# Storing a layer's output earlier, and moving work between PE, VectorE and ScalarE, in a four-layer convolution kernel

## What is computed

```python
x = x + _L0_conv_ref(_gn(x), w_real, w_imag, b_real, b_imag)  # rfft2, complex 3x3 convolution over frequencies, irfft2
x = x + _L1_conv_ref(_gn(x))                                  # gates each row by the sign of a product with column sums
x = x + _L2_conv_ref(_gn(x), L2_conv_W)                       # 3x3 convolution, 16 to 16 channels
x = x + _L3_conv_ref(_gn(x), L3_conv_weight)                  # 3x3 convolution, 16 to 16 channels
```

## Time and profile before

| what | value |
|---|---|
| runs | 4728.77, 4733.0 and 9641.31 us, median 4733.0 |
| profiled execution | 4716.25 us, span 4714.5 us |
| PE busy | 4226.5 us, 90% of the span |
| DVE busy | 3331.8 us, 71% |
| ACT busy | 2541.0 us, 54% |
| DMA | 467.98 MB, mean 99 GB/s; written to HBM 134.22 MB |
| granted PE clock, mean | 0.959 of full speed |

### The profile page before, as it was taken

The page is one execution under the profiler, slowest core; times in us unless marked ns, Lnnn a source line. Parts: engine busy times, 40 slices in busy tenths (PEclk is TensorE's granted clock), DMA queues, the critical chain, the costliest instruction groups (busy, mean ns, idle before and its releaser), DMA issues.

```text
span 4714.5 us, 229091 instructions
## 1 busy us (share of the span) xinstructions
PE 4226.5 (90%) x84848; PEld 2660.6 (56%) x84848; DVE 3331.8 (71%) x13348; ACT 2541.0 (54%) x8637; POOL 1.0 (0%) x6
## 2 busy tenths in 40 slices
PE   4898989989899898998989989899898999988799
PEld 1455765556555566555655556555665556655476
DVE  1887658876588665887658876588756887578873
ACT  4675526655267542775437754377533675335552
POOL 0000000000000000000000000000000000000000
PEclk8999999989999899999999999999999998999999
DMA  7442015520156202661026610356003560034304
GB/s 190 128 136 77 4 40 179 186 82 4 43 184 188 73 4 56 185 187 60 3 66 189 187 46 3 87 184 189 28 3 104 181 185 18 3 99 140 96 4 146
DMA packets 290241, 467.98 MB, mean 99 GB/s; under 512 B 25536, under 2 KB 92288, under 8 KB 289408
## 3 DMA queue, kind: packets, MB, share of 16 engines
q1 hardware_dynamic: 289536, 457.92, 32.2%
HBM read 323.60 MB, written 134.22 MB: 97 GB/s over the span
## 4 chain that ended last, share of the span: by engine, by line
PE 60%; DVE 12%; DMA 8%; issue 8%; SPq 5%; ACT 3%; DVEq 1%; ACTq 1%
PE ps L1352 35%; PE ps L1255 9%; DMA raw<-x 8%; PE ps L1270 4%; PE ps L1263 3%; PE ps L1279 3%; PE ps L1125 2%; DVE shared L858 2%; SPq L426 2%; SPq L433 1%; DVE xin L853 1%; DVE shared L854 1%; ACT x L584 1%; SPq L407 1%; DVE shared L860 1%
## 5 line engine op out<-in xcount | busy, mean ns | idle before, releaser
L1352 PE MATMUL ps<-x,conv_s 32*32 32x512 f32 x49104 | 1753.1, 608 | 76.2 <-DVE x L1016 41.0
L1352 PEld LDWEIGHTS ps<-x,conv_s 32*32 32x32 f32 x49104 | 1246.7, 104 | 520.0 <-issue 290.2
L1255 PE MATMUL ps<-shared 32*32 32x512 f32 x16384 | 654.0, 603 | 0.0
L662 ACT ACTIVATE x<-ps,vec 128x256 f32<-128x256 f32 x512 | 214.6, 470 | 738.6 <-PE ps L1352 738.6
L1270 PEld LDWEIGHTS ps<-hil,shared 128*128 128x128 f32 x4096 | 500.3, 193 | 194.1 <-issue 193.3
L584 ACT ACTIVATE x<-ps,vec 128x128 f32 (+1 forms) x1024 | 376.7, 384 | 430.2 <-PE ps L1270 429.1
L858 DVE SCALAR_TENSOR_TENSOR shared<-xin,trig 128x128 f32<-128x128 f32 x2048 | 530.9, 299 | 106.6 <-DVE shared L854 98.8
L1279 PE MATMUL ps<-eye,vsb 128*128 128x128 f32 x2048 | 369.0, 303 | 222.5 <-DVE vsb L879 127.5
L1270 PE MATMUL ps<-hil,shared 128*128 128x128 f32 x4096 | 567.5, 282 | 0.0
L1086 DVE SCALAR_TENSOR_TENSOR x<-ps,x 128x256 f32<-128x256 f32 x512 | 214.9, 420 | 423.2 <-ACT x L662 422.3
L1255 PEld LDWEIGHTS ps<-shared 32*32 32x32 f32 x16384 | 306.9, 103 | 280.7 <-issue 217.1
(11 more groups left out here) (202 smaller groups left out, 4641.5 us busy)
## 6 DMA issues: line engine op xcount, KB each, us to landing
out<-x SPq DMA_DIRECT2D x512, 256.0 KB
shared<-x SPq DMA_DIRECT2D x448, 256.0 KB
raw<-x SPq DMA_DIRECT2D x256, 256.0 KB
raw<-x SPq DMA_DIRECT2D x512, 128.0 KB
shared<-t_strip SPq DMA_DIRECT2D x512, 96.0 KB, 4.0
x<-x SPq DMA_DIRECT2D x64, 256.0 KB, 7.9
x<-t_proj SPq DMA_DIRECT2D x1, 2048.0 KB, 13.3
trig<-t_trig SPq DMA_DIRECT2D x1, 512.0 KB, 9.9
```

Of the source, the lines that this page charges most:

```text
L1255: mm = pe.matmul(ps[TM * cg:TM * cg + TM, bank, :], wst[TM * rg:TM * rg + TM, k, v, a, :], of[TM * rg:TM * rg + TM, :], start=(a == AXS), ...
L1352: mm = pe.matmul(halves(ps[TM * cg:TM * cg + TM, banks[k], :]), conv_s[TM * rg:TM * rg + TM, kw, second, :], x1b[TM * rg:TM * rg + TM, of, ...
```

## The change

- **Stores.** `DEFERRED` goes from 56 to 8. In the third convolution SP stores 56 strips (all 64 in the last image) in a loop of four stores each; 8 strips are left for the first four pairs of the next first layer. The loads of pairs 0 and 1 of the next image still stand ahead of the stores.
- **PE.** In each step the projection stands between the odd `hilbert` and the odd `turn`, no longer behind both.
- **DVE.** `make_planes` takes the differences first, then the sums, and waits for results less strictly. `x_taken` is counted by the sums, now the second of the two.
- **copy_v.** ACT makes both copies; DVE makes none.

```diff
@@ -27,7 +27,7 @@
 GROUPS = STRIPS // GROUP
 STORE_SEMS = 4
 STORES = 16 * STRIPS // STORE_SEMS
-DEFERRED = STRIPS - 2 * UNROLL
+DEFERRED = 2 * UNROLL
 SIDE = HALF + 2
 WIDE = 2 * SIDE
 PAIRS = STRIPS // 2
@@ -416,14 +416,13 @@
             for k in range(STORE_SEMS):
                 sp.sem_inc(c_stored[k], STORES)
 
-            def store(i, s):
-
-                k = s % STORE_SEMS
+            def store(i, s, k, turn):
+
                 sp.wait_ge(evicted, ev(i, 1 + STRIPS + s + 1))
                 sp.sem_inc(s_sp, 1)
-                sp.wait_ge(c_stored[k], (i + 1) * STORES + s // STORE_SEMS * 16)
+                sp.wait_ge(c_stored[k], (i + 1) * STORES + turn * 16)
                 sp.sem_inc(s_sp, 1)
-                sp.dma_start(out[i].rearrange("c (s r) w -> s r c w", r=ROWS)[s], x1[:, s, 0:N]).then_inc(c_stored[k], 16)
+                sp.dma_start(out[i].rearrange("c (s r) w -> s r c w", r=ROWS)[s], x1[:, bass.ds(s, 1), 0:N]).then_inc(c_stored[k], 16)
 
             def load_next(image, s, t, k):
 
@@ -456,25 +455,19 @@
                     sp.sem_inc(s_sp, 1)
                 for pair in range(2, AHEAD):
                     load_pair(i, pair, 2 * pair)
-                for pair in range(DEFERRED // 2):
+                for pair in range(PAIRS):
                     feed(pair, 2 * pair % TABLES)
-                    if stores_left:
+                    if stores_left and pair < DEFERRED // 2:
                         for e in range(2):
-                            store(i - 1, STRIPS - DEFERRED + pair * 2 + e)
-                for pair in range(PAIRS - UNROLL, PAIRS):
-                    feed(pair, 2 * pair % TABLES)
+                            s = STRIPS - DEFERRED + pair * 2 + e
+                            store(i - 1, s, s % STORE_SEMS, s // STORE_SEMS)
                 if more:
                     for pair in range(2):
                         load_pair(i + 1, pair, 2 * pair)
 
-                for n in range(PAIRS):
-                    if more and n >= PAIRS - (STRIPS - DEFERRED):
-                        sp.wait_ge(evicted, ev(i, 1 + STRIPS + 2 * n + 2))
-                        sp.sem_inc(s_sp, 1)
-                        store(i, n - (PAIRS - (STRIPS - DEFERRED)))
-                    elif not more:
-                        for e in range(2):
-                            store(i, 2 * n + e)
+                with sp.Fori(0, (STRIPS - (DEFERRED if more else 0)) // STORE_SEMS) as j:
+                    for k in range(STORE_SEMS):
+                        store(i, j * STORE_SEMS + k, k, j)
 
             image(0, True, False)
             with sp.Fori(1, B - 1) as i:
@@ -588,8 +581,9 @@
                 def copy_v(pair):
 
                     act.wait_ge(mixed, i * PAIRS + pair + 1 + MIXED_CREDIT)
-                    act.wait_ge(turned, t0 + pair * 2 + T_CREDIT)
-                    nc.scalar.activation(vsb[:, 1, :], ps[:, BV + 1, :], ACT.Identity).then_inc(v_copied[1], 1)
+                    for e in range(2):
+                        act.wait_ge(turned, t0 + pair * 2 - 1 + e + T_CREDIT)
+                        nc.scalar.activation(vsb[:, e, :], ps[:, BV + e, :], ACT.Identity).then_inc(v_copied[e], 1)
 
                 def squares(s, k, uses):
 
@@ -849,17 +843,20 @@
                     dve.wait_ge(x_loaded[e], (i * PAIRS + pair + 1) * (16 + 16 * e))
                     dve.wait_ge(mixed, i * PAIRS + pair - 1 + MIXED_CREDIT)
                     plus, minus = xin[:, k, 0:HALF], xin[:, k, HALF:N]
-                    b.did(V.scalar_tensor_tensor(plus, raw[:, e, 0:HALF], v1(MEAN2), raw[:, e, HALF:N], ALU.subtract, ALU.add))
-                    V.tensor_tensor(minus, raw[:, e, 0:HALF], raw[:, e, HALF:N], ALU.subtract).then_inc(x_taken, 1)
-                    b.then(V.scalar_tensor_tensor(fg(wst[:, k]), fg(mix_s[:, 1]), row_trig[:, 0, bass.ds(s, 1)], fg(mix_s[:, 0]), ALU.mult, ALU.add))
-                    dve.wait_ge(x_taken, i * STRIPS + s + 1 + RAW)
+                    b.did(V.tensor_tensor(minus, raw[:, e, 0:HALF], raw[:, e, HALF:N], ALU.subtract))
+                    V.scalar_tensor_tensor(plus, raw[:, e, 0:HALF], v1(MEAN2), raw[:, e, HALF:N], ALU.subtract, ALU.add).then_inc(x_taken, 1)
+                    b.did(V.scalar_tensor_tensor(fg(wst[:, k]), fg(mix_s[:, 1]), row_trig[:, 0, bass.ds(s, 1)], fg(mix_s[:, 0]), ALU.mult, ALU.add))
+                    b.settle(but=1)
                     for a in range(2):
                         for q in range(2):
                             b.did(V.scalar_tensor_tensor(quarter(planes[:, a, k, :], q, 0), split_in(minus)[:, q, :], 1.0, split_in(trig[:, a, 0:HALF])[:, q, :],
                                                          ALU.mult, ALU.mult, accum_out=gsum[:, 2 * a + q, bass.ds(s, 1)]))
+                        if a == 0:
+                            dve.wait_ge(x_taken, i * STRIPS + s + 1 + RAW)
                         ins = V.tensor_tensor(planes[:, a, k, HALF:N], plus, trig[:, a, 0:HALF], ALU.mult)
                         if a == 0:
                             b.did(ins)
+                            b.settle(but=3)
                             b.did(V.scalar_tensor_tensor(fg(wst[:, k]), fg(mix_s[:, 2]), row_trig[:, 1, bass.ds(s, 1)], fg(wst[:, k]), ALU.mult, ALU.add))
                     ins.then_inc(planes_ready, 1)
                     assert b.n == DVE_B, b.n
@@ -871,12 +868,6 @@
                 c = Steps(dve, d_prep, i * DVE_PREPS)
 
                 t0 = i * STRIPS
-
-                def copy_v(pair):
-
-                    dve.wait_ge(mixed, i * PAIRS + pair + 1 + MIXED_CREDIT)
-                    dve.wait_ge(turned, t0 + pair * 2 - 1 + T_CREDIT)
-                    V.tensor_copy(vsb[:, 0, :], ps[:, BV, :]).then_inc(v_copied[0], 1)
 
                 u0 = i * (STRIPS // UNROLL)
 
@@ -892,7 +883,6 @@
 
                 def step(pair, slot, dotting=True):
 
-                    copy_v(pair)
                     make_planes(i, pair + 2, slot)
                     if dotting:
                         dots(pair - 2)
@@ -904,7 +894,6 @@
                 with dve.Fori(1, PAIRS // 2 - 1) as j:
                     step(j * 2, 0)
                     step(j * 2 + 1, 2)
-                copy_v(PAIRS - 2)
                 dve.wait_ge(b_steps, (t0 + STRIPS) * DVE_B)
                 dve.wait_ge(planes_ready, t0 + STRIPS)
                 dve.wait_ge(dotted, t0 + STRIPS - 8 + DOT_CREDIT)
@@ -918,8 +907,8 @@
                         if j == 1 or kk + 1 < KINDS:
                             c.did(ins)
                 ins.then_inc(f_ready, 1)
+                dve.wait_ge(mixed, i * PAIRS + PAIRS - 1 + MIXED_CREDIT)
                 dots(PAIRS - 4)
-                copy_v(PAIRS - 1)
                 for pair in range(PAIRS - 3, PAIRS):
                     dots(pair)
                 dve.wait_ge(dotted, t0 + STRIPS + DOT_CREDIT)
@@ -1290,10 +1279,11 @@
 
                     mix(t, odd)
                     add_u(t - 1, 1 - odd, table, table_uses)
-                    for e in range(2):
-                        hilbert(t * 2 - 2 + e, e, 1 - odd)
-                        turn(t, e)
+                    hilbert(t * 2 - 2, 0, 1 - odd)
+                    turn(t, 0)
+                    hilbert(t * 2 - 1, 1, 1 - odd)
                     project_next(2 * (1 - odd), table, uses, first)
+                    turn(t, 1)
 
                 pe.wait_ge(v_u, i + 1)
                 pe.wait_ge(a_cols, A_COLS * i + A_COLS)
```

## The result

| | before | after |
|---|---|---|
| median of four runs | 4731.45 us (4728.77 to 4733.0, and one of 9641.31) | 4901.54 us (4892.9 to 4906.85) |
| profiled span | 4714.5 us | 4903.6 us |
| granted PE clock, mean | 0.959 | 0.931 |

The ratio is 1.0352, 95% interval 1.0333 to 1.037. It leaves out the run of 9641.31 us; the two medians alone give 1.036.

A forecast was written before the change was run, and what follows sets the result against it. It took PE's steps in the first layer, with their waits, as the longest part, and SP's order as deciding the seam. Steps -195 us, seams +181, rest 0: 4733 - 14 = 4719, say 4720 us, range 4630 to 4850.

The forecast's parts named there:

- The pace of the stores: At the seam, SP's block of 56 stores: 1.17 us from one store to the next, 65.5 us in all.
- The time of a store, 4.3 us: Wait for the fourth store back: taken from the run's last store, a quarter of it giving 1.08 us a store.
- the source address by register: SP's own work in the new store loop: register addressing and the branch add 0.05 us to 1.12 us a store.
- Rival A: Dearer seam: 1.45 us or more a store through the wait for the fourth store back; 4829 us, chance 0.14.
- Rival C: Stores drain faster at the seams, 0.92 us a strip if SP issues that fast; 4621 us, chance 0.10.
- the page's sum: Seam by the Trainium skill's DMA fit: 56 strips in 34 us, seam free, near 4540 us; part of C's chance.
- The step: First layer, one pair of strips: 8.55 us once PE's waits are covered, from 9.21 and 9.52; -195 us in all.
- rival B: First layer: ScalarE becomes the bound through its second copy, 0.6 us a step; 4845 us, chance 0.06.
- the gap of 5.5 us where SP jumps back: At the seam: time from the last store's end to pair 2's load, kept as before; none from image 0 to 1.
- from SP's load to the mix 13 us: At the seam: pair 2's mix comes 13 us after SP issues its load, with 12 to 16 possible.
- the signs that were named: Profile signs: 65 us store block, steps of 8.5 to 8.7, PE still 20 to 35 at seams, ScalarE idle under 0.9.
- The rest: Outside steps and seams: -1 us an image from planes, +1 us from dense stores in the third convolution, together 0.

The follow-up runs named there:

- half_stores: The changed kernel with each store of the third convolution's loop moving only 256 of 512 columns, except in the last image; 4843.81 us, ratio 1.0229.
- eight_deep: The changed kernel with one wait for evictions per eight stores and eight store semaphores, so a store waits for the eighth before it; 4847.08 us, ratio 1.0224.
- split_wait: `rest_alone` with PE's wait for the odd strip's eviction moved from the start of the mix to its first odd matmuls; 4528.15 us, ratio 0.9554.
- unblocked: The changed kernel with 40 of the 56 stores ahead of the loads of the next image's pair 1; 4591.43 us, ratio 0.9692.
- rest_alone: The changed kernel with SP's program as before the change (`DEFERRED = 56`); 4573.69 us, ratio 0.9652.

## Why the prediction was wrong

It said 4720 us, no change; it is 4901.54, slower by 3.5%, and above the range. The account of the mechanism held: a gain in the first layer, given back at the seam behind a block of 56 stores. Two terms were mis-sized, both towards a faster kernel, and it took both to leave the range: with the seams as measured and the steps as forecast the sum is 4733 - 195 + 286 = 4824, the other way round 4733 - 107 + 181 = 4807, both inside 4630 to 4850.

**The pace of the stores, "I take 1.17".** The blocks take 78.7 to 81.1 us, 1.41 to 1.45 a store, in place of 65.5. That is 13 to 16 us at a seam and 102 in all, nearly the whole difference between +286 and +181. The prediction built the pace from two rows, and both terms were too low. The time of a store, 4.3 us, came from the very last one; with four in flight it is 5.6, which the text had only as the upper end. This term alone gives 1.40, and it did so behind image 0, where SP's own work is 1.14 us, no more than the 1.17 that was forecast. The other term, 0.05 us for "the source address by register", holds there, but behind images 1 to 6, where the image number is in a register as well, it is 0.25: 1.37 in `half_stores`. The trace before already had a loaded store in it. In the last image, with a store each 1.6 us, SP waited twice for the fourth store back, and these had been issued 5.8 and 6.3 us before:

```profile
SPq L425 <- DMA out<-x: 0.6, 2, 0.3
```

**Rival A** has the right pace (1.45) and the right mechanism behind image 0, where waits for the fourth store back make up the 0.27 us between SP's own work and the pace. Behind images 1 to 6 it is one of two limits: SP waits little (3.7 us in the block from image 1 to 2), since its own work is already at 1.37. The argument against A, that a share of 0.50 leaves "a third free" at a store each 1.2 us, fell with `eight_deep`: 1.25 was the least, at a share of 0.53.

**Rival C** and the page's sum are out: with whole strips no block went below 1.25 us a store. By the Trainium skill ("DMA: Bandwidth & Descriptors", the section on the chain of a DMA) the bytes of 56 strips would pass in some 34 us (an estimate from that page, whose fit was measured on DMAs that GpSimd issues; these are SP's). The traces disagree: 81.0 us after, and 70.2 in the fastest block.

**The step, "I take 8.55".** It is 8.85 in image 0 and 9.00 in image 1 (8.98 to 9.02 in images 1 to 6): -107 us, not -195. The waits for ScalarE and VectorE ahead of the transposes did go. The failed step is "With neither wait left the step is PE's own": the text asked what is late next only for ScalarE's copy, not for its eviction, which now ends 0.55 us ahead of the mix. `split_wait` shows it to be 0.2 of the 0.3 us in image 0. In images 1 to 6 it gives 0.15 us, and 0.3 us above the forecast remain that were not resolved.

**What held.** ScalarE's copy costs nothing visible (rival B out); the gap of 5.5 us where SP jumps back (5.4; it was 3.7 in `half_stores`, so it is no constant), and none from image 0 to 1 (0.7); from SP's load to the mix 13 us (13.6); VectorE's 7.1 busy us a step (210.88 / 30 = 7.03); the data rate in the first layer (145 GB/s); image 7 gains nothing; the lower granted clock after the stall (0.50 between 1334 and 1352), seen in the mix at 1352.95, 1.89 us for 1.15. Of the signs that were named, two failed beside the block and the step: PE stood still for 45.20 us at the seam from image 1 to 2, not 20 to 35, and ScalarE, busy for 211.76 of 269.97 us, is idle for 1.9 us in a step, not under 0.9.

**The rest, "I set both against each other".** It is +11 us instead of 0, of which 3 are behind the last image; no run takes it apart.

## What to carry to other kernels

A queue in program order is priced by what stands behind a blocked item: 40 stores moved ahead of one load were worth 310 us, though all bytes and all stores stayed. When a pace has several limits of nearly the same size, take each at its loaded value and expect that relieving one alone shows little. Look at one block in which one of the limits is absent, as that behind image 0 here. The busy share of the DMA engines did not tell how much room was left. After a wait is covered, list the other results that the engine needs in that step and by how much each is early: here the next was late at once.

## What the runs showed of the hardware

- SP's own work for a store with two waits: 1.14 us with the strip in a register and the image a constant, 1.37 with both in registers (address instruction of 74 and 138 ns), 1.12 with the strip a constant.
- A 256 KB store comes back after 4.3 us at the end of the kernel, after 5.4 to 5.8 us with four in flight and after 9.8 to 10.1 with eight. No block of whole strips went faster than 1.25 us a store (`eight_deep`), at a DMA share of 0.53; there the issuing instruction itself took 879 ns instead of 627. Halving the bytes took 1.41 to 1.14 where SP's own work was 1.14, and 1.45 to 1.37 where it was 1.37.
- Where SP goes back in its program after a block of stores, 5.4 us pass to its next issue, 3.7 us with half the bytes and 0.7 us where it goes straight on.
- PE's idle time without a releaser in the convolutions grows with the bytes stored beside them (3.6 us in `half_stores`, 13.1 after, 25.7 in `unblocked`, single stops up to 2.0 us). The rest of the image is 5.5 us longer in `unblocked` than in `rest_alone` (273.3 against 267.8), more than this idle time; after, at 270.5, is not clear of the 270.3 of before.
